# A hand-written end for a streamed six-layer program, and two moves at the seam between its two halves

## What is computed

```python
xn = _layernorm(x, axis=-1)
x = x + causal_attention(xn, ...) + six_layers(xn, ...)

# causal_attention: 16 heads of 64, latent_kv = x @ w_kv_down, kv = latent_kv @ w_kv_up, softmax, @ w_out
# six_layers:
for i in range(DEPTH):                                     # DEPTH = 6
    x = attn_layer(shift_tokens(x), Wqkv[i], ...) + x      # windows of 32, rotary, 16 heads of 64
    x = ffn_layer(shift_tokens(x), ...) + x
# ffn_layer: layer norm, hg = xn @ W1 + b1; a, gate = split(hg); a * gelu(gate) @ W2 + b2, inner width 341
```

## Time and profile before

| what | before |
|---|---|
| median of three executions | 1989.51 us |
| the profiled execution, its own time | 1994.65 us |
| its span, first to last instruction | 1992.9 us |
| between its time and its span | 1.75 us |
| mean granted TensorE clock | 0.985 |
| PE, DVE, ACT, POOL busy | 94%, 79%, 71%, 68% |

### The profile page before, as it was taken

The page is one execution under the profiler, slowest core; times in us unless marked ns, Lnnn a source line. Parts: engine busy times, 40 slices in busy tenths (PEclk is TensorE's granted clock), DMA queues, the critical chain, the costliest instruction groups (busy, mean ns, idle before and its releaser), DMA issues. The chain is left out here.

```text
span 1992.9 us, 68753 instructions
## 1 busy us (share of the span) xinstructions
PE 1876.1 (94%) x27097; PEld 1401.0 (70%) x27097; DVE 1582.2 (79%) x3047; ACT 1408.2 (71%) x2840; POOL 1363.9 (68%) x1442
## 2 busy tenths in 40 slices
PE   4999998899999999999999999999999999999986
PEld 3777765677767777777777677776777777777762
DVE  4777776798888888888888888888888888888763
ACT  3666665578777777777777678777777777777761
POOL 3000023798898787888787978789878789878740
PEclk9999999899999999999999999999999999999995
DMA  3000001344434344334343343343433433334330
GB/s 130 2 1 0 0 0 29 84 105 103 130 86 104 96 103 126 92 91 105 96 127 98 88 106 100 97 129 86 105 97 101 129 93 92 102 96 103 92 91 21
DMA packets 190582, 171.20 MB, mean 86 GB/s; under 512 B 32160, under 2 KB 186440, under 8 KB 190152
## 3 DMA queue, kind: packets, MB, share of 16 engines
q1 hardware_dynamic: 190280, 167.02, 32.0%
HBM read 21.14 MB, written 1.05 MB: 11 GB/s over the span
## 5 line engine op out<-in xcount | busy, mean ns | idle before, releaser
L412 POOL TENSOR_TENSOR z_raw<-rot_u,rot_v 128x256 f32<-128x256 f32 x768 | 552.2, 743 | 111.0 <-DVE rot_v L1120 106.2
L405 POOL TENSOR_TENSOR z_norm<-probs_t,z_raw 128x512 f32<-128x512 f32 x376 | 481.9, 1282 | 91.5 <-DVE probs_t L1160 89.0
L1119 DVE TENSOR_TENSOR rot_u<-bank,tabs 128x512 f32<-128x512 f32 x384 | 262.9, 685 | 168.6 <-ACT sq L573 168.2
L429 POOL TENSOR_TENSOR sqs<-sq 128x512 f32<-128x512 f32 x192 | 246.0, 1281 | 90.6 <-issue 90.3
L888 PE MATMUL bank<-x_high,w_high 128*128 128x256 f32 x768 | 301.7, 393 | 0.2 <-issue 0.2
L604 ACT ACTIVATE pair_bank<-pair_bank 128x512 f32<-128x512 f32 x192 | 111.7, 582 | 217.3 <-DVE pair_bank L1100 217.1
L1120 DVE TENSOR_TENSOR rot_v<-bank,tabs 128x512 f32<-128x512 f32 x384 | 261.2, 680 | 0.0
L573 ACT ACTIVATE sq<-bank 128x512 f32<-128x512 f32 x384 | 225.5, 588 | 49.7 <-PE bank L890 43.4
L879 PEld LDWEIGHTS bank<-probs_t,v_late 128*64 128x64 f32 x3072 | 155.0, 137 | 145.2 <-issue 145.2
L591 ACT ACTIVATE probs_t<-bank 64x512 f32<-64x512 f32 x384 | 226.7, 590 | 42.4 <-PE bank L867 40.2
L841 PE MATMUL bank<-sqs,consts 128*128 128x512 f32 x384 | 199.6, 601 | 24.6 <-POOL sqs L429 24.6
(11 more groups left out here) (168 smaller groups left out, 4563.5 us busy)
## 6 DMA issues: line engine op xcount, KB each, us to landing
zqk<-z_norm SPq DMA_DIRECT2D x1536, 64.0 KB, 2.1
v_late<-v_sb SPq DMA_DIRECT2D x192, 192.0 KB, 2.6
w_qkv<-in_L_ffn_Wqkv SPq DMA_DIRECT2D x18, 512.0 KB, 4.7
v_late<-v_sb SPq DMA_DIRECT2D x192, 32.0 KB, 2.9
wo<-in_L_ffn_Wo SPq DMA_DIRECT2D x24, 128.0 KB, 2.4
w<-in_L_ffn_W SPq DMA_DIRECT2D x12, 170.5 KB, 2.9
consts<-in_constants SPq DMA_DIRECT2D x1, 1088.0 KB, 5.1
w_qkv<-in_L_attn_w_kv_up SPq DMA_DIRECT2D x2, 512.0 KB, 6.2
```

The source lines that it names most:

```text
L405: return pool.tensor_tensor(z_norm[:, parity, idx, :, :], rinv(m)[:, idx, :].unsqueeze(1).broadcast_to([P, 2, T]), z_raw[:, parity, idx, : ...
L412: a = pool.tensor_tensor(z_raw[:, parity, idx, half, :], rot_u[:, idx, half, :], rot_v[:, idx, 1 - half, :], ALU.add)
L429: pool.tensor_tensor(sqs[:, :, :], sq[:, :, 0, :], sq[:, :, 1, :], ALU.add).then_inc(S["sums_ready"], 1)
L1119: dve.tensor_tensor(rot_u[:, idx, :, :], src, tabs[:, 2 * idx, :, :], ALU.mult)
```

## The change

The slots now end at 191 on every engine, and what slots 192 to 205 did is written out by itself. The bodies of the slots are moved into functions (`spread_out`, `deviations`, `project_group`, `residual`, `hidden_out` and others) and are otherwise the same. In the new end

- the up and gate matmuls of the last two pairs go to six different banks instead of `B_M`, the centring, the variance and the down matmuls to three more places;
- the gelu of the last pair reads its gate from PSUM with the bias added in it, so the three copies of the gates are gone;
- DVE makes the sums `xs + attn` of pairs 0 and 1 right after slot 191, pair 2's inside the last MLP; for pair 3 it adds `xs` into `attn` ahead of time, and one instruction then adds MLP output, bias and that sum straight into `xh`;
- the transposes, row sums and output DMAs of pairs 0 to 2 come between the last MLPs' steps;
- on PE the up matmuls of pair 22 and the transposes of pair 0 stand before the output projection of group 191.

At the seam the `project_out` of batch 6 goes to bank `B_N`, waits for `lv_ready` in place of `q_square` and `q_prod`, and DVE copies it from there; the wait for `res_done` moves from `queries(1)` to `norms(0)`. POOL's memset of `spread` moves from the end of its slot 0 to the beginning.

```diff
-FIRST, LAST = -4, GROUPS + 14
+FIRST = -4
...
-            for s in range(LAST):
+            for s in range(GROUPS):
...
+        W, N, L = UNITS - 1, GROUPS - 1, MLPS - 1
+        UP_BANKS, GATE_BANKS, ROW_BANKS = (0, 1, 4), (3, 2, 5), (5, 7, 7, 0)
...
             def slot(s):
                 one, two = active(s, -4, GROUPS - 4), active(s, -3, GROUPS - 3)
+                if s == 0:
+                    pool.wait_ge(S["pv_done"], STEPS)
+                    pool.memset(spread[:, :, :, :], 0.0).then_inc(S["spread_zero"], 1)
...
-                if s == 0:
-                    pool.wait_ge(S["pv_done"], STEPS)
-                    pool.memset(spread[:, :, :, :], 0.0).then_inc(S["spread_zero"], 1)
...
             stream(slot)
+
+            spread_out(N)
+            deviations(W - 1, B_M)
+            output_out(N)
+            gained(W - 1)
+            gelus(L - 1)
+            last_gelus(L - 1)
+            act.preload_act_table_set(LN_EXP)
+            xc_squares(W)
+            deviations(W, bank[2])
+            gained(W)
+            act.preload_act_table(ACT.Gelu)
+            for c in range(3):
+                act.wait_ge(S["gate_done"], 3 * L + c + 1)
+                act.wait_ge(S["hid_ready"], 3 * L - 3 + c + 1)
+                act.activation(gate[0:CW[c], c, :], bank[GATE_BANKS[c]][0:CW[c], :], ACT.Gelu, bias=gate_bias[0:CW[c], c:c + 1]).then_inc(S["gelu_done"], 1)
...
                     if last:
-                        pe.wait_ge(S["q_square"], 1)
-                        pe.wait_ge(S["q_prod"], 1)
-                    project_out(B_Q)
+                        pe.wait_ge(S["lv_ready"], 1)
+                    project_out(B_N if last else B_Q)
...
+            turn_windows(N)
+            project_group(N - 1)
+            weigh_windows(N, W, G - 1, W % 2)
+            pe.wait_ge(S["q_prod"], GROUPS)
+            pe.wait_ge(S["q_square"], GROUPS)
+            for c in range(3):
+                hidden(L - 1, c, 0, bank[UP_BANKS[c]], "up_done")
+            pe.wait_ge(S["k_prod"], GROUPS)
+            pe.wait_ge(S["k_square"], GROUPS)
+            rows(0)
+            project_group(N)
+            pe.wait_ge(S["lres_done"], UNITS)
+            pe.wait_ge(S["ln_var"], W)
+            pe.matmul(bank[3][:, 0:T], con("center"), xs[:, NB - 1, 0:T], start=True, stop=True).then_inc(S["xc_done"], 1)
+            pe.wait_ge(S["xc_squared"], UNITS)
+            pe.matmul(bank[2][:, 0:T], con("avg"), xc2[:, :], start=True, stop=True).then_inc(S["var_done"], 1)
+            for c in range(3):
+                pe.wait_ge(S["hid_ready"], 3 * L - 3 + c + 1)
+                mm = pe.matmul(bank[6][:, :], w2[0:CW[c], c, :], hid[0:CW[c], c, :], start=(c == 0), stop=(c == 2))
+            mm.then_inc(S["mlp_done"], 1)
+            pe.wait_ge(S["ln_done"], GROUPS)
+            rows(1)
+            pe.wait_ge(S["xh_ready"], UNITS)
+            pe.wait_ge(S["ln_var"], UNITS)
+            pe.wait_ge(S["rows_ready"], 1)
+            for c in range(3):
+                hidden(L, c, INNER, bank[GATE_BANKS[c]], "gate_done")
+            for c in range(3):
+                hidden(L, c, 0, bank[UP_BANKS[c]], "up_done")
+            pe.wait_ge(S["rows_ready"], 2)
+            rows(2)
+            pe.wait_ge(S["mlp_res"], L)
+            for c in range(3):
+                pe.wait_ge(S["hid_ready"], 3 * L + c + 1)
+                mm = pe.matmul(bank[6][:, :], w2[0:CW[c], c, :], hid[0:CW[c], c, :], start=(c == 0), stop=(c == 2))
+            mm.then_inc(S["mlp_done"], 1)
+            rows(3)
...
-            dve.wait_ge(S["mlp_res"], MLPS)
+
+            whole(0)
+            whole(1)
+            normed_out(W - 1)
+            residual(W)
+            centred_out(W)
+            for c in range(3):
+                hidden_out(L - 1, c, bank[UP_BANKS[c]], 2 * L - 2 + (2 if c == 2 else 1))
             dve.wait_ge(S["x_in"], 32)
-            for p in range(PAIRS):
-                for rows, at in ((slice(0, 64), 0), (slice(64, P), 1)):
-                    a = dve.tensor_tensor(xh[rows, 2 * p:2 * p + 2, :], xs[rows, 2 * p:2 * p + 2, at:at + T], attn[rows, 2 * p:2 * p + 2, :], ALU.add)
-                a.then_inc(S["fin_sum"], 1)
-            for p in range(PAIRS):
-                dve.wait_ge(S["fin_done"], p + 1)
-                tiles = slice(2 * TT * p, 2 * TT * (p + 1))
-                dve.tensor_tensor(xn_rows[:, tiles, :], bank[p][:, :].rearrange("p (k c) -> p k c", c=P), x_rows[:, tiles, :], ALU.add).then_inc(S["rows_ready"], 1)
+            rows_out(0)
+            normed_out(W)
+            mlp_residual(L - 1, bank[6])
+            last = slice(NB - 2, NB)
+            dve.wait_ge(S["lres_done"], UNITS)
+            for rows, at in ((slice(0, 64), 0), (slice(64, P), 1)):
+                a = dve.tensor_tensor(attn[rows, last, :], xs[rows, last, at:at + T], attn[rows, last, :], ALU.add)
+            a.then_inc(S["rest_sum"], 1)
+            rows_out(1)
+            hidden_out(L, 0, bank[UP_BANKS[0]], 2 * L + 1)
+            whole(2)
+            for c in (1, 2):
+                hidden_out(L, c, bank[UP_BANKS[c]], 2 * L + c + 1)
+            rows_out(2)
+            dve.wait_ge(S["mlp_done"], MLPS)
+            dve.wait_ge(S["rest_sum"], 1)
+            dve.scalar_tensor_tensor(out=xh[:, last, :], in0=bank[6][:, :].rearrange("p (a t) -> p a t", a=2), scalar=out_bias[:, 0:1],
+                                     in1=attn[:, last, :], op0=ALU.add, op1=ALU.add).then_inc(S["fin_sum"], 1)
+            rows_out(3)
```

More of the change, by code:

```diff
@@ L369, in slot @@
                     down_weights(l)
-            for s in range(FIRST, LAST):
+            for s in range(FIRST, GROUPS):
                 slot(s)
@@ L584, in slot @@
                 if four:
[L586 to L592, removed]
+                    spread_out(s - 1)
                 if mlp_slot(s, 17):
@@ L595, in slot @@
                 if normed:
[L596 to L601, removed]
+                    deviations((s - 8) // G, B_M)
                 if three:
@@ L622, in slot @@
                 if g == 3 and active(s, 7, 7 + GROUPS):
[L623 to L626, removed]
+                    xc_squares((s - 7) // G)
                 if normed:
-                    w, b = (s - 8) // G, (s - 8) // G % NB
-                    act.wait_ge(S["xh_raw"], w + 1)
-                    act.activation(xh[:, b, :], xc[:, :], ACT.Identity, bias=gain[:, 1:2], scale=gain[:, 0:1]).then_inc(S["xh_ready"], 1)
+                    gained((s - 8) // G)
                 if four:
[L632 to L635, removed]
+                    output_out(s - 1)
                 for c in range(3):
@@ L643, in slot @@
                 if session:
[L644 to L647, removed]
+                    gelus((s - 16) // (2 * G))
                 if one:
@@ L650, in slot @@
                 if session:
-                    act.activation(gate[0:CW[2], 2, :], gate[0:CW[2], 2, :], ACT.Gelu).then_inc(S["gelu_done"], 1)
+                    last_gelus((s - 16) // (2 * G))
                 l = layer_begun(s, LAYER + 6)
@@ L810, in causal, with project_group @@
                     values(g, g, 0)
+            def project_group(n):
+                og, unit = n % G, n // G
+                pe.wait_ge(S["lyt_ready"], n + 1)
+                if n % LAYER < G:
+                    pe.wait_ge(S[f"wo_in{og}"], 16 * (n // LAYER + 1))
+                if og == 0:
+                    after(pe, "lres_done", unit)
+                if n == 0:
+                    pe.wait_ge(S["res_done"], NB)
+                for c in (2 * og, 2 * og + 1):
+                    mm = pe.matmul(B_X[:, 0:T], wo[:, c, :], yt[:, c, :], start=(c == 0), stop=(c == HD // P - 1))
+                mm.then_inc(S["lwo_done"], 1)
             def project_out(bankx):
@@ new lines, in centred_out, with normed_out, residual @@
+            def centred_out(w):
+                dve.wait_ge(S["xc_done"], w + 1)
+                after(dve, "xh_ready", w)
+                dve.tensor_copy(xc[:, :], B_M[:, 0:T]).then_inc(S["xc_ready"], 1)
+            def normed_out(w):
+                dve.wait_ge(S["rstd_ready"], w + 1)
+                dve.tensor_tensor(xc[:, :], xc[:, :], rstd[:, :], ALU.mult).then_inc(S["xh_raw"], 1)
+            def residual(w):
+                b = w % NB
+                dve.wait_ge(S["lwo_done"], G * (w + 1))
+                for rows, at in ((slice(0, 64), 0), (slice(64, P), 1)):
+                    dst = xs[rows, b, at:at + T]
+                    a = dve.tensor_tensor(dst, B_X[rows, 0:T], dst, ALU.add)
+                a.then_inc(S["lres_done"], 1)
@@ new lines, in hidden_out, with whole @@
+            def hidden_out(p, c, bankx, gelus):
+                dve.wait_ge(S["up_done"], 3 * p + c + 1)
+                dve.wait_ge(S["gelu_done"], gelus)
+                after(dve, "mlp_done", p)
+                dve.scalar_tensor_tensor(out=hid[0:CW[c], c, :], in0=bankx[0:CW[c], :], scalar=out_bias[0:CW[c], 1 + c:2 + c],
```

(7 more changed lines are left out.)

100 lines of the change are left out of this document (58 added, 42 removed).

## The result

| | before | changed |
|---|---|---|
| median, first measurement | 1991.05 us (4 executions) | 1957.91 us (4) |
| ratio of the times, 95% interval | | 0.9832 (0.9814 to 0.9850) |
| median, a later measurement | 1989.75 us (9) | 1959.05 us (5) |
| ratio there | | 0.9846 (0.9830 to 0.9862) |
| span of the profiled execution | 1992.9 us | 1955.5 us |

The change made the kernel faster by 1.7%, 33.1 us on the medians of the first measurement; 1957.0 had been predicted. The two profiles are 37.4 us apart.

A forecast was written before the change was run, and what follows sets the result against it. PE, busy 94% over the span, was taken as the bound, with waiting chains in drain and seam. 27.5 + 7.7 = 35.2 us off the profiled 1994.65 gave 1959.5; allowing for the lower median, 1957 was said, range 1949 to 1969.

The forecast's parts named there:

- The drain's chain: Steps after the last slot product, timed at full clock: span ends at 1963.75 us, 29.1 us earlier.
- The clock in the new drain: New end: 29.1 us saved at full clock, 26.2 if it falls and comes back; 27.5 taken, between these.
- the thin place: New end, 1942.65 to 1945.95 us: PE has only two short matmuls; a clock fall there costs 2.4 to 2.9 us.
- The rival in which it stays at half to the end: New end: clock stays at 1.2 GHz throughout, 9.4 us less gain, 1966 us; chance 15%.
- The clock in the old drain: Old drain: granted clock 0.54, then 0.50; if the median's 5.1 us are clock the change removes, gain about 30 us.
- The seam: Batch 6's projection and POOL's memset, before the slots: 2.2 + 5.5 = 7.7 us saved, carried to the end.
- the memset: POOL at the seam: moved into its idle time, it removes PE's 6.63 us wait before slot 1; 5.5 us gained.
- the projection: Batch 6's at the seam: starts 0.95 us earlier, 1.75 more if the clock holds; 2.2 us taken.
- The slots did not take the gain back: Rival: the first full period of slots absorbs the seam's gain, leaving 27.5 us alone, 1965 us; chance 10%.
- The dearer table switch: ACT in the new end: each table switch costs 2.66 us, not 1.28; end 2.7 us later, 1960 us; chance 3%.
- DVE's order: Rival in the new end: DVE's fixed order holds the chain at each step, 6 us lost, 1963 us; chance 4%.
- The period of the slots: Expected still 65.8 us per eight slots; rival: the 192 slots lock into another period, 2021 us; chance 2%.

The follow-up runs named there:

- the late sums: Changed kernel with all sums, transposes, row sums and output DMAs behind the last MLP residual, last pair's residual as two instructions and two sums: 1964.58 us.
- the filled drain of before: Kernel before with unused short bf16 matmuls on PE ahead of each wait of the drain after slot 192: 1986.16 us, ratio 0.9975.
- the second reordering: Changed kernel with group 191's projection behind pair 22's first up matmul, pair 2's sums, transposes and row sum behind the last products and down matmuls: 1955.83 us.

## Why the prediction was right

**The drain's chain** was right in its steps. By the forecast at full clock, against the profile, counted from the end of the last product: projection of group 191 ends at 4.5 us, measured 4.1; pair 22's down matmuls end at 10.6, measured 10.0; last up at 16.5, 15.6; last down matmul at 20.4, 19.3; end 25.6, 24.2. What it had too long is mostly the handing over between matmuls (I gave each group of three 2.84 us, they took 2.74, with their starts overlapping the one before) and 0.35 us of the output's end.

**The clock in the new drain** was the term that was mis-sized. I took 27.5 us as halfway between a clock that falls at the thin place and one that doesn't. It fell at the thin place in two of the seven profiles of the new end without a reordering (with the projection back in B_Q, 25.9 us in place of 24.2, and with the late sums), so it cost nothing in most profiles, and 1.7 us where it came, where I had 2.9. The rival in which it stays at half to the end did not happen in any of the nine. The Trainium skill (TensorE: Matmul & The Clock Gate, "What's actually happening") says that the default state is throttled and activity releases it; the filled drain of before agrees as far as its last transposes, at 1.00 with matmuls that nobody uses.

**The clock in the old drain** is where the sum and the measurement differ by kind. Against its own profile the gain was 37.4 us where I had 35.2; on the medians it was 33.1. I had said that if the 5.1 us between the profiled execution and the median were clock lost in the places that the change removes, the gain on the median would be about 30 and the time 1959.5. The two measurements of the change gave 33.1 us (1957.91) and 30.7 (1959.05), so both this case and my 1957 fit. For the drain it is supported by 30.5 us in the profile and 25.8 on the median (interval 21.5 to 33.4), and more firmly by the executions sorted by their clock above.

**The seam.** For the memset, 5.5 us were forecast. Between the means of the profiles with and without it the distance from slot 0 differs by 5.5 us at slot 2, 5.4 at slot 16 and 6.1 at slot 191; profiles alike in the memset differ by 3 us or more there, so the last 0.6 may be no more than that. The median of the memset alone gives 4.3. The 1.1 us of idle time before POOL's rotation are what lies between the forecast's 5.5 and PE's own bound of 6.6. The scores of slot 2, which the forecast put near 369.5, began at 371.30: it counted the projection's gain on a clock that starts with the program, and the program had started 2.5 us later. For the projection, 2.2 us were forecast; its own steps stand in every profile (0.83 us of idle time, 1.69 where the clock had fallen), but no median shows them. That the clock had fallen because of the idle stretch, as the forecast put it, is not the whole of it: with the new end alone the same stretch was followed by an unbroken clock.

**The rivals.** The slots did not take the gain back (memset alone). The dearer table switch is refuted by the rows: the switch at 1932.42 takes 1.28 us and the gelu follows at once (1933.72). DVE's order costs 0.51 us before pair 2's transposes and some tenths before the norm, and the second reordering, which moves pair 2's sums and transposes out of the way, ends the last down matmuls 1.1 us earlier: far from the 6 us of that rival. The period of the slots stayed: slot 16 to slot 24 takes 65.6 us in the profile after, 65.8 before.

**Luck.** The forecast lay 0.9 us from the first measurement, and that is closer than its parts were. Against its own profile the drain gained 30.5 us where I had 27.5, and the rest 6.9 where I had 7.7; the subtraction for the long profiled execution, 2.5 us, was a choice between two cases. Two measurements of the same change differ by 2.4 us, so a hit within 1 us owes something to chance. The steps were right; the last two or three microseconds were not known.

## What to carry to other kernels

When a pipeline written slot by slot runs out of work, its drain becomes a chain of single steps, and TensorE's clock can fall on top of it (here to a mean of 0.60 to 0.69 over the drain): write the end out by itself, spread it over the banks that are free, and move into its gaps what was waiting for the very end. Look on each engine for a step that nobody is waiting for yet but that stands in front of one who is (here a memset of under 1 us, behind a slot's whole work, cost 5.5 to 6 us in the profiles, 4.3 on the median). Before pricing a gain from one profile, ask how much of the price is clock, since that part changes from execution to execution; here it was, by the medians, some 5 of 30 us.

## What the runs showed that I had not expected

- The same old drain took 50.9, 54.7 and 56.1 us in three profiles, at a mean granted clock of 0.69, 0.62 and 0.60 and with the same busy time of DVE and ACT, and the new one 24.19, 24.20 and 24.21 in three.
- The start of the program differs too: the queries of group 0, in code that no experiment touches, began between 304.3 and 307.3 us.
- Filling PE's waits with unused matmuls made the old kernel 0.25% faster (0.9960 to 0.9990), though it adds work to the engine that is busiest over the span.
